# Gated cross-attention with an expert feed-forward: queries and keys taken from raw, pre-transposed inputs

## The reference, cut to what matters

```python
xl = (x - mean(x)) / sqrt(var(x) + 1e-5)                 # layernorm over 512
xn = xl * rsqrt(mean(xl**2) + 1e-6) * (1 + rms_scale)
mn = ctx * rsqrt(mean(ctx**2) + 1e-6) * (1 + rms_scale)
q = rope(xn @ q_w) * 128**-0.5                           # 4 heads of 128, positions 64..1087
k = rope(mn @ k_w); v = mn @ v_w                         # one key and value head, positions 0..63
p = softmax(where(mask, q @ k.T, -2.38e38))              # over 64 context rows
x1 = x + tanh(g_xattn) * (p @ v) @ out_w
out = x1 + tanh(g_ffn) * ffn(layernorm(x1))
```

## Time and profile before

| what | us |
|---|---|
| median of 3 runs | 1845.2 |
| lowest and highest run | 1835.22, 1848.7 |
| profiled execution | 1833.57 |
| its span | 1831.8 |
| TensorE busy (share of the span) | 1702.0 (93%) |
| VectorE, ScalarE, GpSimd busy | 1401.2, 880.0, 472.3 |
| mean granted TensorE clock | 0.988 of full speed |

### The profile page before, as it was taken

The page is one execution under the profiler, slowest core; times in us unless marked ns, Lnnn a source line. Parts: engine busy times, 40 slices in busy tenths (PEclk is TensorE's granted clock), DMA queues, the critical chain, the costliest instruction groups (busy, mean ns, idle before and its releaser), DMA issues.

```text
span 1831.8 us, 54306 instructions
## 1 busy us (share of the span) xinstructions
PE 1702.0 (93%) x23728; PEld 1236.6 (68%) x23728; DVE 1401.2 (76%) x2102; ACT 880.0 (48%) x1146; POOL 472.3 (26%) x773
## 2 busy tenths in 40 slices
PE   6999999999999999989999999999999999999964
PEld 4777777777777777776576657656665765676541
DVE  5788888888888888737778777777877877787757
ACT  5443444333444434445655565465556556554621
POOL 3455555555555555410110011011001100110100
PEclk9999999999999999999999999999999999999987
DMA  9523233333333323254775686567567656855661
GB/s 303 170 105 128 105 136 110 130 115 135 111 129 116 129 105 128 116 196 177 253 257 199 231 285 217 198 242 266 200 239 258 251 182 240 288 204 214 243 231 69
DMA packets 128393, 339.53 MB, mean 185 GB/s; under 512 B 13856, under 2 KB 20768, under 8 KB 110752
## 3 DMA queue, kind: packets, MB, share of 16 engines
q1 hardware_dynamic: 116928, 254.28, 39.4%
q10 hardware_dynamic: 11232, 81.79, 12.2%
HBM read 259.49 MB, written 76.55 MB: 183 GB/s over the span
## 4 chain that ended last, share of the span: by engine, by line
PE 87%; ACT 5%; issue 4%; DVE 3%; DMA 0%; SPq 0%; POOL 0%; DVEq 0%; POOLq 0%; ACTq 0%
PE ps L774 19%; PE ps L1230 14%; PE ps L838 10%; PE ps L1202 8%; PE ps L1257 8%; PE ps L209 6%; PE ps L1272 4%; PE ps L195 4%; PE ps L1252 3%; PE ps L804 3%; PE ps L787 3%; ACT gat L1078 2%; PE ps L825 2%; PE ps L816 1%; PE ps L872 1%
## 5 line engine op out<-in xcount | busy, mean ns | idle before, releaser
L1118 DVE STREAM_TRANSPOSE res<-res 128x2048 f32<-128x2048 f32 x128 | 292.0, 2294 | 0.1
L1073 ACT ACTIVATE gat<-ps 128x1536 f32<-128x1536 f32 (+1 forms) x128 | 172.2, 1345 | 214.2 <-PE ps L1202 214.2
L177 POOL TENSOR_TENSOR b_va<-b_mv,eps_layer 128x2 f32<-128x2 f32 x64 | 12.6, 197 | 845.7 <-DVE b_mv L168 844.9
L774 PE MATMUL ps<-xTh,qh 128*128 128x512 f32 x512 | 208.1, 406 | 0.6 <-DVE qs L623 0.6
L774 PE MATMUL ps<-xTh,ql 128*128 128x512 f32 x512 | 200.0, 391 | 0.0
L774 PE MATMUL ps<-xTl,qh 128*128 128x512 f32 x512 | 199.9, 390 | 0.0
L1141 DVE COPY res<-ps 128x1024 f32<-128x1024 f32 x128 | 156.7, 1224 | 46.6 <-PE ps L1257 46.5
L1083 ACT ACTIVATE res<-ps 128x1024 f32<-128x1024 f32 x128 | 131.2, 1025 | 102.2 <-PE ps L1257 102.2
L1202 PE MATMUL ps<-sel,xin 32*128 32x128 f32 x4096 | 152.8, 283 | 24.9 <-ACT sel L237 13.6
L1202 PEld LDWEIGHTS ps<-sel,xin 32*128 32x128 f32 x4096 | 128.9, 186 | 59.8 <-ACT gat L1073 39.1
L838 PE MATMUL ps<-vw,pTh 128*128 128x512 f32 x512 | 165.5, 404 | 0.0
(11 more groups left out here) (129 smaller groups left out, 3352.4 us busy)
## 6 DMA issues: line engine op xcount, KB each, us to landing
gat<-in_W ACTq DMA_DIRECT2D x48, 1024.0 KB, 7.9
xin<-in_x SPq DMA_DIRECT2D x64, 512.0 KB, 3.7
x_scratch<-xin SPq DMA_DIRECT2D x64, 512.0 KB, 2.8
xin<-x_scratch SPq DMA_DIRECT2D x64, 512.0 KB, 4.1
xin<-x_scratch SPq DMA_DIRECT2D x128, 256.0 KB, 5.8
out<-xin SPq DMA_DIRECT2D x128, 256.0 KB, 3.8
xh<-in_W SPq DMA_DIRECT2D x25, 1024.0 KB, 5.1
xin<-in_W SPq DMA_DIRECT2D x25, 1024.0 KB, 5.1
```

What stands on the lines that cost most here:

```text
L774: last = e.matmul(ps[:, 2 + n % 2, :], a[:, c, n * DH:(n + 1) * DH], b[:, c, :], start=(k == 0), stop=(k == len(parts) - 1))
L1073: e.activation(o, v, ACT.Copy).then_inc(m_gaA.sem, 1)
L1118: e.transpose(v, v).then_inc(m_tr.sem, 1)
```

## The change: what it does, and the diff

The host hands over `x` and the context a second time, transposed (`xT`, `ctxT`). The transposes of x and of the context on TensorE, with the normed copies that fed them, go. The raw transposed unit is loaded by DMA into `xT` (one buffer, 1 MB); `hi` copies from it on ScalarE, and `lo` subtracts on GpSimd, where it stands in the queue around `rotated(g+1, 1)`. The mean of x is taken out by subtracting from the scaled query weights their mean over the features (a product with a matrix of 1/512 and four subtractions, ahead of the loops). The scale of a token goes into the exponential, which becomes two instructions a half; the scale of a context row goes into the logits (`kscale`) and into the eviction of the values (`gr`). Loads ahead of the loops are issued in another order, the statistics run two units ahead in place of three, and the turning of the keys stands in the loop over `k`. The diff, cut:

```diff
-        xh = sb0("xh", [P, TH, D])
-        ring = [xh[:].rearrange("p n d -> p (n d)"), xin[:, 3].rearrange("p n d -> p (n d)")]
+        xT = sb0("xT", [P, C, HT])
+        ring = [xT[:].rearrange("p c t -> p (c t)"), xin[:, 3].rearrange("p n d -> p (n d)")]
...
+        kscale = sb("kscale", [P, 2, NC])
+        mean_of = qs[:, 0, 0:P]
...
+        turned_x = lambda u: xT_in[u // 2].rearrange("(c p) t -> p c t", p=P)[:, :, u % 2 * HT:(u % 2 + 1) * HT]
...
+            e.dma_start(rs1[:], rms).then_inc(d_rs.sem, 16)
+            for k in range(2):
+                e.dma_start(kvraw[:, :, k * DH:(k + 1) * DH], kv_w[k, 0].rearrange("(c p) h -> p c h", p=P)).then_inc(d_kvw.sem, 16)
+            for c in range(C):
+                e.dma_start(mnT[:, c], ctxT_in[c * P:(c + 1) * P]).then_inc(d_ctxT[c].sem, 16)
+            for n in range(H):
+                e.dma_start(qraw[:, :, n, :], q_w[n].rearrange("(c p) h -> p c h", p=P)).then_inc(d_qw.sem, 16)
+            e.dma_start(ow, out_w.rearrange("n h d -> h n d")).then_inc(d_ow.sem, 16)
...
+            for t in range(NC // 2):
+                e.dma_start(cx[:, 2 * t:2 * t + 2], ctx_in.rearrange("b s d -> (b s) d").rearrange("(n p) d -> p n d", p=P)[:, 2 * t:2 * t + 2]).then_inc(d_ctx[t].sem, 16)
             e.dma_start(cos[:], cos_in).then_inc(d_tab.sem, 16)
             e.dma_start(sin[:], sin_in).then_inc(d_tab.sem, 16)
-            e.dma_start(ow, out_w.rearrange("n h d -> h n d")).then_inc(d_ow.sem, 16)
-            for u in range(RING):
+            e.dma_start(xT[:], turned_x(0)).then_inc(d_xT.sem, 16)
+            for u in range(2):
                 for h in range(2):
                     v = slice(2 * h, 2 * h + 2)
                     e.dma_start(xin[:, u, v], unit_tokens(x, u)[:, v]).then_inc(d_x[u][h].sem, 16)
-            for o, v in const_loads:
-                e.dma_start(o[:], v).then_inc(d_const.sem, 16)
-            e.wait_ge(m_kvs.sem, m_kvs.at(0, C - 1))
-            e.dma_start(b2w[:], b2_dram).then_inc(d_b2.sem, 16)
+                if u == 0:
+                    for o, v in const_loads:
+                        e.dma_start(o[:], v).then_inc(d_const.sem, 16)
+                    e.dma_start(b2w[:], b2_dram).then_inc(d_b2.sem, 16)
+            e.wait_ge(m_ksc.sem, m_ksc.at(0, 1))
+            e.dma_start(kscale[S:P, 0], kscale[0:S, 0]).then_inc(d_ksc.sem, 16)
+            e.dma_start(kscale[0:S, 1], kscale[S:P, 1]).then_inc(d_ksc.sem, 16)
             e.wait_ge(m_kr.sem, m_kr.at(0, 1))
...
+                if k == 7:
+                    e.wait_ge(m_lo.sem, m_lo.at(0, C - 1))
+                    e.dma_start(xT[:], turned_x(1)).then_inc(d_xT.sem, 16)
+            for u in range(2, RING):
+                for h in range(2):
+                    v = slice(2 * h, 2 * h + 2)
+                    e.dma_start(xin[:, u, v], unit_tokens(x, u)[:, v]).then_inc(d_x[u][h].sem, 16)
             e.wait_ge(m_vl.sem, m_vl.at(0))
             e.dma_start(vraw[:], vw_dram[1]).then_inc(d_vr.sem, 16)
             for k in range(VB):
                 e.wait_ge(d_vws[k].sem, d_vws[k].at(B // VB - 1, 1))
-            e.wait_ge(d_const.sem, d_const.at(0, 7))
+            e.wait_ge(m_lo.sem, m_lo.at(1, C - 1))
+            e.dma_start(xT[:], turned_x(2)).then_inc(d_xT.sem, 16)
...
+                    if h == 0 and unit(u + 3):
+                        e.wait_ge(m_lo.sem, m_lo.at(u + 2, C - 1))
+                        e.dma_start(xT[:], turned_x(u + 3)).then_inc(d_xT.sem, 16)
...
+            def lo(u, c):
+                e.wait_ge(m_hi.sem, m_hi.at(u, c))
+                e.tensor_tensor(xTl[:, c, :], xT[:, c, :], xTh[:, c, :].bitcast(F32), ALU.subtract).then_inc(m_lo.sem, 1)
+
+            for c in range(C):
+                lo(0, c)
+            for c in range(C):
+                e.wait_ge(m_qhi.sem, m_qhi.at(0, c))
+                e.tensor_tensor(ql[:, c], qraw[:, c].rearrange("p n h -> p (n h)"), qh[:, c].bitcast(F32), ALU.subtract).then_inc(m_qlo.sem, 1)
             norm_scale(0)
...
                     e.tensor_tensor(vw[:, b % 2, 1], vraw[:], vw[:, b % 2, 0].bitcast(F32), ALU.subtract).then_inc(m_vl.sem, 1)
+                if unit(g + 2):
+                    lo(g + 2, 0)
+                    lo(g + 2, 1)
                 if unit(g + 1):
                     rotated(g + 1, 1)
-                if unit(g + 3):
-                    norm_scale(g + 3)
+                if unit(g + 2):
+                    lo(g + 2, 2)
+                    lo(g + 2, 3)
+                    norm_scale(g + 2)
...
             def hi(u, c):
-                e.wait_ge(m_T.sem, m_T.at(u, c))
-                e.activation(xTh[:, c, :], ps[:, c % 2, :], ACT.Copy).then_inc(m_hi.sem, 1)
+                e.wait_ge(d_xT.sem, d_xT.at(u))
+                if u:
+                    done = m_Q.at(u - 1, H - 1) if c == C - 1 else m_Qc.at(u - 1, c)
+                    e.wait_ge(m_Q.sem if c == C - 1 else m_Qc.sem, done)
+                e.activation(xTh[:, c, :], xT[:, c, :], ACT.Copy).then_inc(m_hi.sem, 1)
 
             def logits(u):
                 e.wait_ge(m_L.sem, m_L.at(u))
-                e.activation(lt[:], ps[:, 3:5, :], ACT.Identity, scale=float(DH) ** -0.5,
+                if u == 0:
+                    e.wait_ge(d_ksc.sem, d_ksc.at(0, 1))
+                e.activation(lt[:], ps[:, 3:5, :], ACT.Identity, scale=kscale[:, u // 2 % 2, u // 4:u // 4 + 1],
                              bias=fill[:, u // 2:u // 2 + 1]).then_inc(m_lt.sem, 1)
...
-            def normed(u):
-                e.wait_ge(m_nrm.sem, m_nrm.at(u, 8))
-                if u:
-                    e.wait_ge(m_T.sem, m_T.at(u - 1, C - 1))
-                for t in range(TH):
-                    last = e.activation(xh[:, t, :], xin[:, u % RING, t, :], ACT.Identity,
-                                        scale=sc[:, u % RING, t:t + 1], bias=nb[:, u % RING, t:t + 1])
-                last.then_inc(m_xh.sem, 1)
...
-            for t in range(NC):
-                e.wait_ge(m_ms.sem, m_ms.at(0, 4 * (t // 4) + 3))
-                e.activation(cx[:, t, :], cx[:, t, :], ACT.Copy, scale=rr[:, t:t + 1]).then_inc(m_cn.sem, 1)
-            for h in range(2):
-                for c in range(C):
-                    e.wait_ge(m_cT.sem, m_cT.at(0, h * C + c))
-                    e.activation(mnT[:, c, h * HT:(h + 1) * HT], ps[:, 2 * c + h, :], ACT.Copy).then_inc(m_mn.sem, 1)
...
+            e.wait_ge(m_ms.sem, m_ms.at(0, 7))
+            e.activation(gr[:], rr[:], ACT.Copy, scale=gate_x[:]).then_inc(m_gr.sem, 1)
+            e.wait_ge(m_gr.sem, m_gr.at(0))
             for k in range(B):
                 e.wait_ge(m_vwp.sem, m_vwp.at(k // 2, k % 2 * 2))
                 if k >= VB:
                     e.wait_ge(d_vws[k % VB].sem, d_vws[k % VB].at(k // VB - 1, 1))
-                e.activation(vwb[:, k % VB, 0, :], ps[:, 4 + 2 * (k % 2), :], ACT.Copy, scale=gate_x[:]).then_inc(m_evA.sem, 1)
-                if k in T0_AFTER:
-                    for c in T0_AFTER[k]:
-                        hi(0, c)
+                e.activation(vwb[:, k % VB, 0, :], ps[:, 4 + 2 * (k % 2), :], ACT.Copy, scale=gr[:, k // 2:k // 2 + 1]).then_inc(m_evA.sem, 1)
+                if k in (1, 3, 5, 7):
+                    hi(0, k // 2)
+                if k in (8, 10, 12, 14):
+                    c = k // 2 - 4
+                    e.wait_ge(m_qct.sem, m_qct.at(0, c))
+                    e.activation(qh[:, c], qraw[:, c].rearrange("p n h -> p (n h)"), ACT.Copy).then_inc(m_qhi.sem, 1)
...
+                    e.wait_ge(m_nrm.sem, m_nrm.at(g, 6))
                     for tp in range(2):
                         e.wait_ge(m_sb.sem, m_sb.at(g, tp))
-                        e.activation(lg[:, tp, :], lg[:, tp, :], ACT.Exp).then_inc(m_ex.sem, 1)
+                        for t in range(2):
+                            v = lg[:, tp, 2 * t * P:2 * (t + 1) * P]
+                            last = e.activation(v, v, ACT.Exp, scale=sc[:, g % RING, 2 * tp + t:2 * tp + t + 1])
+                        last.then_inc(m_ex.sem, 1)
                 u = g + 2
-                if unit(u):
-                    normed(u)
                 b = (g + 1) // 2
...
-            def lo(u, c):
-                e.wait_ge(m_hi.sem, m_hi.at(u, c))
-                e.tensor_tensor(xTl[:, c, :], ps[:, c % 2, :], xTh[:, c, :].bitcast(F32), ALU.subtract).then_inc(m_lo.sem, 1)
...
+                values_lo(h)
+            e.wait_ge(m_ms.sem, m_ms.at(0, 7))
+            for o in range(2):
+                v = slice(o * S, (o + 1) * S)
+                e.tensor_scalar(kscale[v, o], rr[v], float(DH) ** -0.5, None, ALU.mult).then_inc(m_ksc.sem, 1)
+            e.wait_ge(m_qm.sem, m_qm.at(0))
             for c in range(C):
                 v = qraw[:, c].rearrange("p n h -> p (n h)")
-                e.tensor_scalar(v, v, rs1[:, c:c + 1], None, ALU.mult).then_inc(m_qsc.sem, 1)
-            for t in range(TH):
-                stats(0, t)
-            moments(0)
```

(95 more changed lines are left out.)

132 lines of the change are left out of this document (39 added, 93 removed).

## The result

The changed kernel takes 1851.27 us (median of 20 runs, 1844.76 to 1858.31) where the one before, in the same sessions, takes 1843.16. The ratio is 1.0044, with a 95% interval of 1.0024 to 1.0064: some 8 us slower, 4 to 12 by the interval. The forecast was 11 us slower. Of 1.74 us of TensorE's work that each round lost, nothing reached the time.

The account below looks back on a forecast made before the run. TensorE's issue was taken to bound each round, until GpSimd's rotation came late for `logits`. Loops +3.9, round 30 +0.3 and ahead of the loops +7 made +11 us on the 1845.2 median: 1856 us, range 1822 to 1880.

Parts of the forecast that it names:

- The wait in front of `logits`: TensorE ahead of `logits(g+1)`, waiting for the rotated queries: 1.29 us in even rounds, 1.93 in odd ones.
- The slack of 0.45 us: Between GpSimd's rotation ending at 405.78 and `logits` starting at 406.27, less 0.04 us handover; subtracted from the 1.74 us removed.
- GpSimd's queue: Two `lo` of 1.26 us each ahead of `rotated(g+1, 1)`; in odd rounds L491 stands ahead of them too.
- Just in time: Even rounds: two `lo` end at 403.1, just ahead of the rotation's 403.23; no further wait, but no room.
- The exponential: Two instructions a half, scale from memory, 0.93 us instead of 0.63: the sum starts later, +0.26 us a round.
- The new transfer: `xT` of unit u+3, 1 MB landing in 5 to 8 us before `hi`: costs nothing, some 5 us to spare.
- Ahead of the loops: Keys ready at 37.4 instead of 31.89 us, SyncE's chain +5.5, two `lo` in round -1 +1.5: together +7 us.
- The sum of the terms: Whole kernel: +3.9 us in the loops, +0.3 in round 30, +7 ahead of the loops, +11 in all.
- Nobody waits: Rival in the loops: rotation in time, the whole -52 us shows, some -5 ahead; 1788 us, 6%.
- Cheap parts: Rival: loops give -7 us and the part ahead of them -5; 1833 us, 18%.
- all three of its parts: Of the 1833 us rival: `lo` at 1.03 us, the exponential free, and SyncE's chain ahead of the loops not later.
- GpSimd slower than alone: Rival in GpSimd's queue between L491 and `rotated(g+1, 1)`: `lo` at 1.7 us beside VectorE, 25 us more; 1881 us, 19%.

Follow-up runs that it names:

- the short rotation: The changed kernel with the rotation's second pair on GpSimd cut from 512 to 8 columns (output not the reference's): 1804.44 us, ratio 0.9796 to the kernel before.
- values 2 first: The changed kernel with `rotated(g+1, 1)` ahead of the first two `lo` and values 2 moved ahead of `logits`: 1803.48 us, ratio 0.9798 to the kernel before.
- the rotation first: The changed kernel with `rotated(g+1, 1)` ahead of the first two `lo` in GpSimd's queue: ratio 1.0012 to the kernel before.
- the experiment: One 512-column exponential a half, in the changed kernel with `rotated(g+1, 1)` before `lo` and values 2 before `logits`: 20.54 for 20.74 us a round, ratio 0.9778.

## Why the prediction was right

**The wait in front of `logits`.** Predicted 1.29 and 1.93 us. TensorE's idle time is 1.21 and 1.80; its matmul ends are modelled, and counted in starts, as the prediction did, the wait is what a round has over 20.74 us: 1.27 and 1.87. Rounds predicted at 22.01 and 22.65, measured at 22.02 and 22.61. That the wait is the whole loss of the loops is shown by the kernels with the short rotation and with values 2 first: both give 20.74 us, the 22.20 less 1.74 plus 0.28 for the exponential in two. The slack of 0.45 us, read from one end and one start in the earlier trace rows, carried the forecast.

**GpSimd's queue.** A `lo` has 1.29 us and a step of 1.25, by L475 as taken. "Just in time" in even rounds is what the chain has: `lo` ends at 414.27 and the rotation starts at 414.37. With the rotation first the odd rounds lose their extra, as the sum had it.

**The exponential.** Predicted +0.26 a round, against one exponential without a scale; measured +0.28 in the 36 products. The 0.20 of the experiment is against one exponential with a scale and leaves out what the scale costs. That an odd round's wait takes the delay back is borne out too: with one exponential the odd rounds stay at 22.6 us. The chain of an odd round does come over the first and second `turned` into the first rotation, which the text left out, but that rotation starts 12.68 us after `logits` with the pair and 12.63 with one, so it moves by 0.05 us.

**The new transfer.** Predicted at nothing, with 1 MB landing in 5 to 8 us. In the loops it landed in 5.0 to 7.5 us, and no `hi` waited for it.

**Ahead of the loops.** Predicted: keys at 37.4, last eviction at 64, `logits(0)` at +7. Measured: 39.3, 64.05, +7.5. The keys were 2 us later than predicted. The sum had ScalarE's first copy of `ow` at 17.5 us and GpSimd through with `owl` at 23.8; that copy stood behind an instruction that waited for the small loads until 19.54, and GpSimd was through at 25.81. SyncE needed less time behind the keys (the eight stores from place 4 to 7 are out at 60.5 us, 7.20 us for eight in place of 7.7). These two errors are against each other, so that 64 came out is in part luck. And what released the last eviction was TensorE, at a low clock, not the store that the prediction named, though the evictions at 48.57 and 59.07 did wait for stores. Behind it, the first `turned` starts 5.7 us later than before, through `b2` as predicted, and the second 6.2, since TensorE's queries are later by then; the second pair of the rotation adds 1.4, where 1.5 were predicted.

**What was not in it.** The low clock in that part: about 1.7 us at `logits(0)`, and, ahead of it, the 12 products at 5.49 us in place of some 2.8 (an estimate, from 51 in 11.98), of which about 0.5 us reached `logits(0)`, by the starts of the first and second `turned`. The sum of the terms, +11, against +13 in the profiles and +8 in the times: the size is right to within what either tells, and no closer.

**The rivals.** Nobody waits: refuted. Cheap parts: refuted, all three of its parts. GpSimd slower than alone: refuted in this kernel, with 36 of L503 between 1277 and 1297 ns and all 128 of L492 between 1253 and 1311, but the effect is real: it came at once when VectorE got two SBUF inputs.

## What to carry to other kernels

Before work is taken from the engine that is always busy, look at what it stands in front of. In an in-order queue it covers the latency of whatever comes behind it, and only the slack there (one end and one start in the timeline) is sure gain. When the wait appears, fill it with work that is already in the queue just behind, and check first that the waiting work isn't cheap only because it runs whole.

## What the hardware did that was not expected

Eight of the 64x64 products with 512 columns took 1.93 us in the timeline where they use two quarters of the array at a time, and sixteen took 1.95 us where they use four.

TensorE's granted clock fell to 0.50 in the five microseconds from 60 and from 80 us, after stretches in which it waited for stores and for GpSimd, and 16 instructions of `logits` took 3.73 us there in place of 1.95. Waits of 1.2 to 1.8 us in each round left it at 1.00. With the low parts on VectorE the wait ahead of `logits` was 2.03 us at 392, 417, 440 and 464 us, and the clock fell behind it in some rounds and not in others: 0.58 in the four microseconds from 392, 1.00 in those from 416.

Two `tensor_tensor` of 128x512 on VectorE with both inputs in SBUF took 2.37 us beside GpSimd's `tensor_tensor`, which took 1.66 and 1.71 in place of 1.3, and 1.27 us with GpSimd idle.
